# Slot attention in a Flamingo-like block: exponentials normalised per token, gates read from PSUM, and a new order of the steps

## The reference, cut to what matters

```python
Pn = rmsnorm(P, input_norm_w)                       # context, 77 keys
k_proj, v_proj = Pn @ Wk.T, Pn @ Wv.T
for _ in range(3):
    sn = rmsnorm(slots, slot_norm_w)
    scores = (sn @ Wq.T) @ k_proj.T * d ** -0.5
    attn = softmax(scores, axis=-2)                 # over the tokens
    attn = attn / (sum(attn, axis=-1) + 1e-6)       # per token, over the keys
    updates = attn @ v_proj
    gi, gh = updates @ wi.T + bi, slots @ wh.T + bh # three gates of 128 columns each
    r, z = sigmoid(gi_r + gh_r), sigmoid(gi_z + gh_z)
    n = tanh(gi_n + r * gh_n)
    slots = (1 - z) * n + z * slots
```

## Time and profile before

| | |
|---|---|
| median of 3 runs | 316.64 us (316.25 to 316.88) |
| the profiled execution, its own time | 317.1 us |
| its span | 315.3 us |
| PE busy | 296.9 us (94%) |
| DVE busy | 231.4 us (73%) |
| ACT busy | 149.2 us (47%) |
| POOL busy | 63.7 us (20%) |
| granted PE clock, mean | 0.998 |

### The profile page before, as it was taken

The page is one execution under the profiler, slowest core; times in us unless marked ns, Lnnn a source line. Parts: engine busy times, 40 slices in busy tenths (PEclk is TensorE's granted clock), DMA queues, the critical chain, the costliest instruction groups (busy, mean ns, idle before and its releaser), DMA issues.

```text
span 315.3 us, 5757 instructions
## 1 busy us (share of the span) xinstructions
PE 296.9 (94%) x2088; PEld 199.5 (63%) x2088; DVE 231.4 (73%) x670; ACT 149.2 (47%) x330; POOL 63.7 (20%) x95
## 2 busy tenths in 40 slices
PE   8899999998899999999999999999999997998963
PEld 3463453793436488888888365589788774666431
DVE  4882985789768389796796495465558569999995
ACT  0448255422555864542306637523426538876411
POOL 5242454334100001000303301010311502211020
PEclk9999999999999999999999999999999999999999
DMA  6970300002200000000000000000000000000002
GB/s 185 309 248 0 102 13 3 0 2 75 73 0 2 0 2 0 3 0 2 0 0 2 3 1 2 0 2 0 0 2 0 2 1 0 3 0 0 3 0 67
DMA packets 8976, 8.73 MB, mean 28 GB/s; under 512 B 3547, under 2 KB 6901, under 8 KB 8949
## 3 DMA queue, kind: packets, MB, share of 16 engines
q1 hardware_dynamic: 8949, 8.37, 8.7%
HBM read 7.84 MB, written 0.52 MB: 27 GB/s over the span
## 4 chain that ended last, share of the span: by engine, by line
PE 65%; DVE 21%; ACT 6%; issue 3%; POOL 2%; DMA 2%; DVEq 0%; SPq 0%; ACTq 0%
PE psum L996 59%; DVE wide L1901 3%; DVE mx L1734 3%; ACT wide L1396 3%; PE psum L1090 2%; DMA early<-in_ffn 2%; DVE xn_t L1919 1%; DVE xn L1921 1%; DVE q L1914 1%; DVE wide L1908 1%; DVE wide L1907 1%; PE psum L1128 1%; DVE nmax L1868 1%; PE psum L1176 1%; PE psum L1184 1%
## 5 line engine op out<-in xcount | busy, mean ns | idle before, releaser
L934 POOL TENSOR_TENSOR nw<-mv,minus_half 128x2 f32<-128x2 f32 x32 | 22.2, 708 | 143.5 <-DVE mv L1597 143.5
L1396 ACT ACTIVATE wide<-psum 128x512 f32<-128x512 f32 x72 | 37.0, 607 | 14.9 <-PE psum L996 14.7
L1734 DVE TENSOR_REDUCE mx<-psum 128x4 f32<-128x308 f32 x96 | 38.6, 471 | 6.0 <-PE psum L996 5.9
L1396 ACT ACTIVATE q<-psum 128x512 f32<-128x512 f32 (+1 forms) x30 | 17.8, 597 | 36.0 <-PE psum L996 28.1
L996 PE MATMUL psum<-q_hi,first_hi 128*128 128x512 f32 (+1 forms) x68 | 30.6, 450 | 0.0
L996 PE MATMUL psum<-wide 78*128 78x386 f32 (+1 forms) x69 | 25.5, 507 | 3.0 <-DVE wide L1885 1.9
L996 PE MATMUL psum<-q_lo,first_hi 128*128 128x512 f32 (+1 forms) x68 | 26.8, 394 | 0.0
L996 PE MATMUL psum<-q_hi,first_lo 128*128 128x512 f32 (+1 forms) x68 | 26.7, 393 | 0.0
L996 PEld LDWEIGHTS psum<-early,wide 128*128 128x128 f32 x192 | 24.7, 191 | 2.3 <-ACT wide L1396 0.5
L996 PE MATMUL psum<-halves 128*128 128x512 bf16 x102 | 25.8, 379 | 0.0
L996 PE MATMUL psum<-early,wide 128*128 128x128 f32 x192 | 25.4, 276 | 0.1
(11 more groups left out here) (230 smaller groups left out, 562.8 us busy)
## 6 DMA issues: line engine op xcount, KB each, us to landing
early<-in_ffn SPq DMA_DIRECT2D x8, 256.0 KB, 4.8
w_attn<-in_attn SPq DMA_DIRECT2D x1, 640.0 KB, 7.4
w_attn<-in_attn SPq DMA_DIRECT2D x2, 288.0 KB, 6.4
x<-in_x SPq DMA_DIRECT2D x2, 256.0 KB, 3.6
w_ffn<-in_ffn SPq DMA_DIRECT2D x1, 512.0 KB, 7.2
early<-in_ffn SPq DMA_DIRECT2D x1, 512.0 KB, 3.7
out<-x SPq DMA_DIRECT2D x2, 256.0 KB, 2.3
rows<-in_rows SPq DMA_DIRECT2D x1, 468.0 KB, 6.1
```

The source lines that it names most:

```text
L934: G.tensor_tensor(nw[:, b, 2, tiles], mv[:, b, tiles, 1], minus_half[:, tiles], ALU.pow)\
L1396: A.activation(dst, banks.bank(*name)[0:rows_, 0:cols_], fn, **kw).then_inc(drained["act"], 1)
L1734: last = V.tensor_reduce(mx[:, b, t, lane_heads(g)], banks.bank("max", layer, b, t, g)[:, 0:GK].rearrange("p (h k) -> p h k", k=CTX), AX.X ...
```

## The change

It computes the same. The attention weights are now normalised before the last product, and the gates are summed in PSUM:

- `slot_inverse` only inverts the sums over the tokens. New `token_sums`: four PE products with one moving column (those inverses) give each token's sum over the keys; DVE inverts them as 128x4. New `token_spread`: four PE products, with the inverse broadcast as the stationary operand and the identity as the moving one, lay them out as keys x tokens; DVE multiplies ex by both into `ex_n` (78x512).
- `hidden` writes units gr, gz, gh; for gh a product of two rows adds the bias bh first (`bias_parts`, f32r, high part and rest). Nothing copies them out.
- `gru` is now three units of four products with 128 columns of the unscaled `vw`: r and z add onto gr and gz in PSUM, n goes to a unit gn of its own.
- ACT takes tanh of r and of z from PSUM, 512 columns each; DVE makes n's argument from gh and gn in PSUM in `gru_n`, two halves of two instructions; `gru_z` is once over 512 columns.
- `slots_in` 5 prepares the bias once, five small DVE instructions.
- Some planner costs and all of `LATER` change, and with them the order of all engines.

```diff
-        0: (-33, 31, -1, -544, 402, 47, 152, -17, -56, -25, 945, -17, -75, 156, 927, -52, -32, -827, 963, -40, 976,
+        0: (-2665, 640, 0, -324, 76, 830, 1188, 905, -27, 39, 7, 0, 966, -360, 0, -507, -44, -99, 478, 0, 958, -1733,
...
@@ half_steps
-            reader = "act" if i < 2 else "dve"
-            step("hidden", it, i, after=[at("act", "slots_turn", it, 1), prepared("act", "slots_in", 4)]
-                 + in_order("pe", "hidden", it, i), then={"act": in_order("act", "hidden", it, i)}, pe=0.89,
-                 **{reader: 0.54 if i < 2 else 0.6})
-        step("slot_inverse", it, after=[at("act", "slot_scores", it), prepared("act", "slots_in", 3)], dve=0.57)
-        for t in range(T):
-            step("gru", it, t, after=[at("dve", "slot_inverse", it)] + in_order("pe", "gru", it, t), pe=0.65)
...
+            step("hidden", it, i, after=[at("act", "slots_turn", it, 1), at("pe", "slot_scores", it), prepared("dve", "slots_in", 5)]
+                 + in_order("pe", "hidden", it, i), pe=0.89 if i < 2 else 1.11)
+        step("slot_inverse", it, after=[at("act", "slot_scores", it)], dve=0.17)
+        step("token_sums", it, after=[at("dve", "slot_inverse", it)], pe=0.5, dve=0.18)
+        step("token_spread", it, after=[at("dve", "token_sums", it)], pe=0.9, dve=0.68)
+        for i in range(3):
+            step("gru", it, i, after=[at("dve", "token_spread", it), at("pe", "hidden", it, min(i, 1)), prepared("act", "slots_in", 3)]
+                 + in_order("pe", "gru", it, i), pe=0.89)
+        step("gru_r", it, after=[at("pe", "gru", it, 0)], act=0.53)
+        step("gru_z", it, after=[at("pe", "gru", it, 2)], act=1.28, dve=0.6)
         for h in range(T // 2):
...
+            step("gru_n", it, h, after=[at("act", "gru_r", it), at("pe", "hidden", it, 2), at("pe", "gru", it, 1)]
+                 + in_order("dve", "gru_n", it, h), dve=0.84)
+            step("gru_end", it, h, after=[at("dve", "gru_n", it, h)] + in_order("act", "gru_end", it, h),
+                 then={"dve": [at("dve", "gru_z", it)] + in_order("dve", "gru_end", it, h)}, act=0.34, dve=0.8)
...
@@ norm, stage 7
-            step("integers", after=[at("dve", "norm_end", stage, 1)], dve=0.85)
-            step("rounded", after=[at("dve", "integers")], dve=0.65)
+            step("integers", after=[at("dve", "norm_end", stage, 1)], dve=0.99)
+            step("rounded", after=[at("dve", "integers")], dve=0.44)
...
@@ PE, hidden
+                bk = start_unit(("gr", "gz", "gh")[i], it, b)
...
+                if i == 2:
...
+                    mm(bk[:, :], ones[:, 0:1].broadcast_to([2, P]), bias_parts[:, :].unsqueeze(1).broadcast_to([2, T, D]), stop=False)
@@ PE, new steps
+            def token_sums(b, it):
...
+                for t in range(T):
+                    last = mm(bk[:, t:t + 1], ex[0:KEYS, b, t * P:(t + 1) * P], nmax[0:KEYS, b, 2:3])
+            def token_spread(b, it):
...
+                for t in range(T):
+                    last = mm(bk[0:KEYS, t * P:(t + 1) * P], route_s[:, b, 1, t:t + 1].broadcast_to([P, KEYS]), ident)
...
+                gate = (0, 2, 1)[i]
...
+                for t in range(T):
+                    last = mm(bk[:, t * P:(t + 1) * P], ex_n[0:KEYS, b, t * P:(t + 1) * P],
+                              vw[0:KEYS, b, gate * D:(gate + 1) * D], start=i == 1, stop=i == 1 or t == T - 1)
@@ ACT
+                A.activation(tr[:, b, :, :].rearrange("p t d -> p (t d)"), banks.bank("gr", it, b), ACT.Tanh, scale=0.5)\
...
+                A.activation(tz[:, b, :, :].rearrange("p t d -> p (t d)"), banks.bank("gz", it, b), ACT.Tanh, scale=0.5).then_inc(drained["act"], 1)
@@ DVE
+                V.scalar_tensor_tensor(ex_n[0:KEYS, b, :], ex[0:KEYS, b, :], nmax[0:KEYS, b, 2:3],
+                                       banks.bank("tb", it, b)[0:KEYS, :], ALU.mult, ALU.mult).then_inc(drained["dve"], 1)
...
+                first = V.scalar_tensor_tensor(n_in, n_in, 1.0, banks.bank("gh", it, b)[:, at_], ALU.add, ALU.mult)
...
+                last = V.scalar_tensor_tensor(n_in, n_in, 0.5, banks.bank("gn", it, b)[:, at_], ALU.mult, ALU.add)
```

More of the change, by code:

```diff
@@ L98 @@
 KEYS = CTX + 1
-UPDATE = 3 * D + 2
 PARTED = (1, 3, 5)
@@ L276, in prepare_steps @@
     step("slots_in", 4, after=[at("pe", "slots_in", 4)], dve=0.2)
+    step("slots_in", 5, after=[at("act", "slots_in", 4)], dve=0.9)
 def half_steps(b, step):
@@ L590, in finished_by @@
         return units_of("hidden2", b, args)
-    if phase == "gru_pair":
-        return [unit for t in pair(args[1]) for unit in units_of("gru", b, (args[0], t))]
+    if phase == "hidden":
+        return units_of("hidden", b, args) if args[1] == 2 else []
+    if phase == "gru":
+        return units_of("gru", b, args) if args[1] == 1 else units_of("hidden", b, (args[0], args[1] // 2))
+    if phase in ("gru_r", "gru_z"):
+        return units_of("hidden", b, (args[0], 0 if phase == "gru_r" else 1))
+    if phase == "gru_n":
+        return units_of("hidden", b, (args[0], 2)) + units_of("gru", b, (args[0], 1)) if args[1] else []
     return units_of(phase, b, args)
@@ L1371, in _ @@
                     "down2": down2, "slots_turn": slots_turn, "hidden": hidden, "slot_products": slot_products,
-                    "slot_scores": slot_scores, "gru": gru, "quantised": quantised}
+                    "slot_scores": slot_scores, "token_sums": token_sums, "token_spread": token_spread, "gru": gru,
+                    "quantised": quantised}
             pe.wait_ge(idle_made, 1)
@@ new lines, in token_sums, with token_spread @@
+            def token_sums(b, it):
+                dve.wait_ge(*banks.full("ts", it, b))
+                V.reciprocal(route_s[:, b, 1, :], banks.bank("ts", it, b)[:, 0:T]).then_inc(drained["dve"], 1)
+            def token_spread(b, it):
+                dve.wait_ge(*banks.full("tb", it, b))
+                V.scalar_tensor_tensor(ex_n[0:KEYS, b, :], ex[0:KEYS, b, :], nmax[0:KEYS, b, 2:3],
+                                       banks.bank("tb", it, b)[0:KEYS, :], ALU.mult, ALU.mult).then_inc(drained["dve"], 1)
@@ new lines, in gru_n @@
+            def gru_n(b, it, h):
+                tiles, at_ = slice(2 * h, 2 * h + 2), slice(2 * h * P, (2 * h + 2) * P)
+                if h == 0:
+                    dve.wait_ge(*banks.emptied("gr", it, b))
+                    dve.wait_ge(*banks.full("gh", it, b))
+                    dve.wait_ge(*banks.full("gn", it, b))
+                n_in = flat(tr[:, b, tiles, :])
+                first = V.scalar_tensor_tensor(n_in, n_in, 1.0, banks.bank("gh", it, b)[:, at_], ALU.add, ALU.mult)
+                if h == 0:
+                    link(first)
+                else:
+                    first.then_inc(drained["dve"], 1)
+                    dve.wait_ge(*banks.emptied("gh", it, b))
+                last = V.scalar_tensor_tensor(n_in, n_in, 0.5, banks.bank("gn", it, b)[:, at_], ALU.mult, ALU.add)
+                last.then_inc(n_in_ready[b] if h == 0 else drained["dve"], 1)
@@ L1916, in gru_end, with gru_z @@
+            def gru_z(b, it):
+                dve.wait_ge(z_ready[b], it + 1)
+                V.tensor_tensor(kept[:, b, :, :], tz[:, b, :, :], slots[:, b, :, :], ALU.mult)
             def gru_end(b, it, h):
@@ L1956, in _ @@
                     "back_shared": back_shared, "up": up, "weigh": weigh, "router": router, "choice_turn": choice_turn,
-                    "choose": choose, "slot_products": slot_products, "slot_scores": slot_scores, "hidden": hidden,
-                    "slot_inverse": slot_inverse, "gru_pair": gru_pair, "gru_r": gru_r, "gru_z": gru_z, "gru_end": gru_end,
+                    "choose": choose, "slot_products": slot_products, "slot_scores": slot_scores,
+                    "slot_inverse": slot_inverse, "token_sums": token_sums, "token_spread": token_spread, "gru_n": gru_n,
+                    "gru_z": gru_z, "gru_end": gru_end,
                     "slots_back": slots_back,
```

155 lines of the change are left out of this document (67 added, 88 removed), and 88 rows, old and new, of the table LATER.

## The result

The changed kernel takes 322.95 us (median of four runs, 322.27 to 324.53; the kernel before, beside it, 316.76): 1.021 times as long, interval 1.0189 to 1.0232. It is slower, as forecast, but by 6.2 us where 1.8 stood, and outside the range (313.4 to 320.9). The profiled execution is one of 323.58 us with a span of 321.1.

The account below looks back on a forecast made before the run. The prediction took DVE to bound the slots' stage before and PE after the change: +5.2 us on PE and -3.4 in the tail made +1.8, so 318.4 us from 316.6, with a range of 313.4 to 320.9.

Parts of the forecast that it names:

- DVE was the bound: Slots' stage before the change: DVE bound, busy 27.6 of 28.5 us from 265 to 293.5; PE short of it.
- The sums: token_sums on PE, four one-column products: 0.81 us a unit, by the gating product's row with 17 columns.
- The tail: From the last update to half 1's row maximum: 9.5 us instead of 12.9, 3.4 us less.
- The gaps: PE standing still in the slots' stage after the change: 2.8, 2.7 and 1.7 us, sum 7.2.
- Rival 2: Slots' stage: the halves interleave, only 2.2 of 7.2 us of PE gaps stay, 313.4 us; chance 24%.
- Rival 3: Slots' stage: PE units wait for PSUM banks held until the gates are read, 2.5 us more, 320.9; chance 15%.
- the price of PE's new units: Sums, spread, bias and larger updates on PE: +2.0 us per half and iteration, 9.06 instead of 7.1.
- the upstream order: New order of the first 226 us: costed at nothing, with +-1 us.
- the bias matmul: PE's product adding bh in hidden: 0.23 us, as an f32r product of 512 columns.
- The sign named for it: If the first slots' transpose doesn't start within 1 us of 226.9, the upstream part is wrong.
- DVE's busy time in that window: From 226 us to the last update: DVE's busy time should fall by some 20 us.

Follow-up runs that it names:

- before_dve: The kernel before without three of four reciprocals of the tokens' sums on DVE (tiles 1 to 3 take tile 0's): 314.54 us, ratio 0.9942.
- after_load: The change with the fillers of half 1's third iteration and four extra one-column products ahead of each iteration's first recurrent unit: 326.49 us, ratio 1.0317.
- warm: The change with two filler products ahead of token_sums and two ahead of token_spread in half 1's third iteration: 322.47 us, ratio 1.0186.
- no_bias: The change without the PE product that adds the bias bh (left out of the candidate gate), same order: 319.64 us, ratio 1.0105.
- warm_spread: The change with two filler products ahead of half 1's third token_spread alone: 322.14 us, ratio 1.0175.
- few_sums: The change with one of the four one-column products in each token_sums (three tiles take the first's sums): 319.25 us, ratio 1.0088.
- late_split: The kernel before with ACT's steps split 0 and out_bias moved behind max_rows, as in the change: 317.26 us, ratio 1.0024.
- early_split: The change with warm_spread's fillers and ACT's steps out_bias and split 0 put back ahead of max_rows: 321.28 us, ratio 1.0153.

## Why the prediction was half right

**Right.** DVE was the bound (before_dve) and PE is now (the chain, after_load). From 265 to 293.5 us DVE is busy 17.4 us where it was 27.6. The sums cost by the product, not the column: 0.87 us, for which 0.81 was taken by the row with 17 columns. The tail was put at 9.5 us and is 9.1 in the change's profile, 9.4 in warm. The gaps nearly held: 64.7 us of work and 7.2 of gaps were to make a stage of 71.9, and at full clock it is 74.5 (warm). Summed start to start in warm's timeline, fillers and waits are some 6.2 us of it, 1.0 less than walked, and the same units as counted, 64.6 us at the forecast's prices, take 3.6 more. That is an estimate, since a wait can't be told from a dearer unit everywhere. Rival 2 (closed gaps, under 3 us) falls with that. Rival 3 (banks) shows nowhere in the stage: PE's visible waits there sum to 1.4 us, all for DVE's nmax, products and route_s.

**Wrong.** The steps that failed are two terms of the sum, the price of PE's new units (1) and the upstream order at nothing (2); the clock (3) stands in no term, and (4) was wrong without a price. The sum lies 4.4 us too low, and no one of them alone would have done that.

1. *"the bias matmul 0.23 (as 128.49 - 128.26 for an f32r product of 512 columns)"*. It was priced from the middle of a run of equal products. Between units of f32 it costs 0.51 (no_bias): 6 x 0.28 = 1.7 us of the miss. The sums add 6 x 0.06 = 0.4. The remaining 0.5 us is what is left of some 1.5 us more on other units, most of them beside one of another form (0.97 to 1.00 instead of 0.89 us), against 1.0 us less of gaps; no run took these apart.
2. *"Upstream ... I cost it at nothing, with +-1 us"*. It costs 0.95 us in the first stretch, by a collision of POOL and DVE and a wait for ACT that the windows from 100 us on couldn't show, since they lie at 20 us; and some 0.3 us from half 1's first transposes to half 0's first slots' transposes (201.3 to 201.8 us in the six profiles of the kernel before and its variants, 201.6 to 202.2 in the eleven of the change), not tried. The sign named for it, the first slots' transpose within 1 us of 226.9, held (226.87), by luck: this profile's maxima came 0.93 us earlier than before's (17.66 and 18.59 us), which hid the 0.95.
3. The clock. No step of the prediction holds it; all durations were taken at full clock: 1.7 us in some three of eight runs.
4. *"DVE's busy time in that window should fall by some 20 us"*. It fell by 12 in the stage (52.3 and 40.4 us) and by 15.5 with the end. The sum took each instruction at its mean duration, but those of a row overlap: the 24 scalings of line 1901 have a mean of 613 ns and keep DVE busy for 13.7 us, not 14.7, and the reciprocals between them 154 ns and 2.7 us, not 3.7. It cost nothing, since DVE is not the bound now.

So 1.8 + 2.6 + 0.95 + 0.3 - 0.1 (the tail, as in warm) = 5.55 us, where the change with fillers at full clock (warm_spread, 322.14) is 5.5 above the kernel before; the clock goes with the rest of 6.2. The price of the bias is shown by no_bias, that of the sums by few_sums, the first stretch by late_split and in part by early_split, the clock by warm; the dearer units beside another form, the fewer gaps and the 0.3 us are only read from timelines. No run took the new order, but for two steps of ACT, apart from the new instructions.

As to the trade itself: 15.5 us off DVE's busy time for 12 us on PE (14 with bias and sums as measured) was a loss, since PE had only the 14 us that lay off the chain. Sums, spread and the larger updates all stand in the chain from exp to the gates.

## What to carry to other kernels

Idle time of an engine is a budget only for work off the chain: the same 0.85 us unit cost 0.2 us behind the scores and 0.7 ahead of them. Price a new product by where it will stand, between what neighbours, not by the inside of a run of its own kind. And when an order is made anew, compare distances between two marks in the early stretches too; one instruction of four at 1305 ns instead of 284, with a wait of 0.3 us ahead of it, was worth a sixth of the result, and a start time that agreed by chance hid it. A sum of mean durations overstates what an engine gains where its instructions overlap.

## What the runs showed of the hardware

- The granted clock fell to 0.50 for some 3.5 us after two waits of 0.33 and 0.37 us with one-column products between them, in both profiles of the change (a third run of eight has the same mean clock, 0.99); with two more bf16 fillers in the second wait the mean clock of all four runs was 0.998 or more.
- A DVE TENSOR_SCALAR of 128x128 (0.28 us) took 1.305 us beside POOL's TENSOR_TENSOR of 128x512 (1.33 us), and three copies of 128x32 took 1.24 us instead of 0.33; DVE's reductions from PSUM over the same instruction kept their pace.
- A product of two rows by 512 columns cost 0.51 us between f32 units, more than two products of 128 by 128 (0.44); in a run of its own kind one of 512 columns took 0.23.
- Four f32 products of one moving column took 0.87 us, four of 128 columns 0.89; one alone took 0.20.
